# Groups of two images in place of four, two pursuit chains three steps apart, coefficients scattered by index

## What is computed

```python
g = sigmoid(gate)
x = x + conv2d(gn(x), tern(w), b) + g * conv2d(gn(x), tern(w_child), b_child)   # 3x3, per-channel norm
D = dictionary / (norm(dictionary, axis=0) + EPS)          # [512, 256]: 32 channels * 4 * 4, 256 atoms
X = patches of gn(x), 4x4, [512, 256 per image]
G = D.T @ D + DIAG_EPS * eye;  h_bar = h = (D.T @ X).T
for k in 1..5:
    index = argmax(abs(h) * ~mask)                         # greedy choice of an atom
    # one more row of a Cholesky factor, then the coefficients x_stack of the chosen atoms
    h = h_bar - x_stack @ G[I]
coeffs[b, I] = x_stack
x = x + fold(D @ coeffs)
```

## Time and profile of the kernel before

| | |
|---|---|
| median of 3 runs | 606.79 us |
| profiled execution | 606.02 us, span 604.2 us |
| VectorE busy | 522.8 us, 87% |
| TensorE busy | 457.3 us, 76%, mean granted clock 0.90 |
| ScalarE busy | 310.6 us, 51% |
| GpSimd busy | 222.0 us, 37% |
| chain that ended last | DVE 54%, PE 24%, issue 8% |

### The profile page before, as it was taken

The page is one execution under the profiler, slowest core; times in us unless marked ns, Lnnn a source line. Parts: engine busy times, 40 slices in busy tenths (PEclk is TensorE's granted clock), DMA queues, the critical chain, the costliest instruction groups (busy, mean ns, idle before and its releaser), DMA issues.

```text
span 604.2 us, 7708 instructions
## 1 busy us (share of the span) xinstructions
PE 457.3 (76%) x1778; PEld 319.7 (53%) x1778; DVE 522.8 (87%) x2507; ACT 310.6 (51%) x682; POOL 222.0 (37%) x269
## 2 busy tenths in 40 slices
PE   0198949897659587889985897999964646896955
PEld 0034935365558344567873445677942535674643
DVE  4493579999999999999998999989988999989980
ACT  3544564874662757656576495557122523452212
POOL 3000045243004756471036655620347375404330
PEclk9999988998889699999997897989985877898868
DMA  6979024986000368640304241121113111211113
GB/s 105 172 116 147 17 61 90 163 136 109 1 1 17 88 140 145 118 94 27 70 2 104 69 104 36 35 71 35 36 47 91 36 54 53 69 36 35 35 36 69
DMA packets 108189, 43.40 MB, mean 72 GB/s; under 512 B 103408, under 2 KB 103920, under 8 KB 108144
## 3 DMA queue, kind: packets, MB, share of 16 engines
q1 hardware_dynamic: 102000, 26.13, 25.8%
q0 software_dynamic: 6144, 16.79, 10.7%
HBM read 34.24 MB, written 8.65 MB: 71 GB/s over the span
## 4 chain that ended last, share of the span: by engine, by line
DVE 54%; PE 24%; issue 8%; SPq 4%; ACT 4%; DMA 3%; POOL 1%; DVEq 0%
PE h L395 13%; DVE picked L1054 11%; DVE junk L967 10%; DVE junk L964 9%; PE back_ps L395 7%; DVE top_i L912 7%; DVE top L906 4%; PE conv_ps L395 4%; SPq L246 3%; DMA rows<-gram,idx_u 1%; DVE mask L979 1%; ACT diag L637 1%; POOL rows L352 1%; SPq L253 1%; DMA d_sb<-in_L_conv_dictionary 1%
## 5 line engine op out<-in xcount | busy, mean ns | idle before, releaser
L395 PE MATMUL h<-rows,diag 128*128 128x256 f32 x640 | 173.8, 435 | 85.9 <-ACT diag L637 54.7
L352 POOL DMA_INDIRECT rows<-gram,idx_u x128 | 128.6, 1005 | 215.2 <-DVEq L952 185.6
L395 PEld LDWEIGHTS h<-rows,diag 128*128 128x128 f32 x640 | 137.8, 220 | 124.9 <-DMA rows<-gram,idx_u 58.4
L366 POOL TENSOR_TENSOR picked<-picked 128x256 f32<-128x256 f32 x120 | 88.4, 740 | 146.2 <-DVEq L1058 139.0
L637 ACT ACTIVATE diag<-ident,dx 128x128 f32<-128x128 f32 x320 | 96.8, 389 | 62.9 <-DVEq L1041 49.6
L628 ACT ACTIVATE score<-h 128x512 f32<-128x512 f32 x80 | 47.3, 594 | 113.5 <-PE h L395 103.7
L1054 DVE TENSOR_SCALAR picked<-iota,idx_last,x_last 128x256 f32<-128x256 f32 x160 | 85.3, 569 | 1.5 <-DVE picked L1054 0.9
L967 DVE SCALAR_TENSOR_TENSOR junk<-mask,rows 128x256 bf16<-128x256 bf16 x224 | 82.5, 434 | 0.0
L906 DVE MAX8 top<-score 128x8 f32<-128x256 f32 x160 | 64.5, 415 | 16.5 <-ACT score L628 13.2
L395 PE MATMUL h<-d_sb,z 128*128 128x256 f32 x256 | 63.2, 408 | 9.2 <-DVEq L897 8.3
L395 PEld LDWEIGHTS h<-d_sb,z 128*128 128x128 f32 x256 | 61.1, 328 | 11.4 <-issue 9.2
(11 more groups left out here) (148 smaller groups left out, 580.9 us busy)
## 6 DMA issues: line engine op xcount, KB each, us to landing
xa<-in_x SPq DMA_DIRECT2D x64, 128.0 KB
out<-x SPq DMA_DIRECT2D x64, 128.0 KB
xb<-in_x SPq DMA_DIRECT2D x42, 128.0 KB
rows<-gram,idx_u POOLq DMA_INDIRECT x128
xb<-in_x SPq DMA_DIRECT2D x14, 120.0 KB
rows<-in_x SPq DMA_DIRECT2D x6, 128.0 KB, 4.2
d_sb<-in_L_conv_dictionary SPq DMA_DIRECT2D x4, 128.0 KB, 3.8
gram<-coef_t SPq DMA_DIRECT2D x1, 256.0 KB, 2.2
```

The costliest lines, as they stand in the source:

```text
L352: pool.indirect_dma_start(out=rows[s][:, k, t, :], out_offset=None, in_=gram_dram[:, :], in_offset=bass.IndirectOffsetOnAxis(ap=idx_u[s][: ...
L366: last = nc.gpsimd.tensor_tensor(picked[:, m % 2, t, 0, :], picked[:, m % 2, t, 0, :], picked[:, m % 2, t, j, :], ALU.add)
L395: return nc.tensor.matmul(dst, lhs, rhs, start=start, stop=stop, skip_group_check=skip)
```

## The change

Images go in 8 groups of two; group g is in chain g % 2. The two chains are no longer at the same step: a list `ORDER` of (g, k), which all engines follow, has (g,2) (g+1,0) (g,3) (g+1,1) (g,4) (g+1,2) (g+2,0) (g+1,3) and so on, with two steps of the first group alone at the start and two of the last alone at the end. Front work of group g+2 and back work of group g-3 hang on the entries of the list.

The rows of coefficients (L1054), their sums (L366), their transposes and their copy are gone, except for the last group, whose rows are built by DVE and transposed as before. Instead, DVE computes a place for each coefficient, and POOL writes the coefficients to a zeroed matrix in DRAM with 20 indirect DMAs for each of 7 groups, one coefficient for each of 128 patches (`scatter`). SP zeroes that matrix (`store_zeros`) and loads it already transposed (`load_coef`). 

The convolution's result is kept as `x1[:, image, column mod 4, patch]`, so that `out_conv` writes with a stride and `correlate` and `reconstruct` read without one; 12 images are kept, and results go out through a buffer `y` of two images. The sums of the norms of group g+1 (second norm) and g+3 (first norm) are taken in one call and copied from PSUM by ACT (`copy_sums`). `select` looks at k+1 candidates instead of 8. The gathered rows have a semaphore for each tile, for which `update` and `extract` wait tile by tile. Two images instead of four are prepared before the first correlate, and the dictionary is loaded after the first two.

The core of the diff:

```diff
-    IMG_R = 4
-    ROUNDS = IMAGES // IMG_R
+    SLOTS = 2
+    PAIR = 2
+    GROUPS = IMAGES // PAIR
+    RING = SLOTS * PAIR
+    KEPT = 12
...
+    even = [(g, k) for g in range(0, GROUPS, 2) for k in range(STEPS)]
+    odd = [(g, k) for g in range(1, GROUPS, 2) for k in range(STEPS)]
+    ORDER = even[0:2]
+    for i in range(len(odd) - 2):
+        ORDER += [even[i + 2], odd[i]]
+    ORDER += odd[len(odd) - 2:]
+    LAST = GROUPS - 1
...
+        coef_dram = nc.dram_tensor("coef", [IMAGES * PLACES, 1], F32, kind="Internal").ap()
...
+            for g, k in ORDER:
+                front, back = g + 2, g - 3
+                if k == 0:
+                    load_after(2 * front + RING)
+                    if back >= 0:
+                        store(2 * back)
+                    store_zeros(g + 2)
+                elif k == 1:
+                    load_after(2 * front + 1 + RING)
+                    if back >= 0:
+                        store(2 * back + 1)
+                    if g >= 2:
+                        load_coef(2 * (g - 2))
+                elif k == 2 and g == LAST:
+                    store(2 * (g - 2))
+                    store(2 * (g - 2) + 1)
+                elif k == 3 and g == LAST:
+                    load_coef(2 * (g - 1))
+                elif k == 4 and g >= 1:
+                    load_coef(2 * (g - 1) + 1)
...
+            def scatter(g, first, last):
+
+                s, r = g % 2, g // 2
+                pool.wait_ge(x_last_ready[s], r + 1)
+                pool.wait_ge(zeros_stored[s], 16 * (r + 1))
+                for i in range(first, last):
+                    t, j = divmod(i, STEPS)
+                    pool.indirect_dma_start(out=coef_dram[:, :],
+                                            out_offset=bass.IndirectOffsetOnAxis(ap=place[s][:, t, j:j + 1], axis=0),
+                                            in_=x_last[s][:, t, j:j + 1], in_offset=None
+                                            ).then_inc(scattered[2 * s + t // 2], 16)
...
-                        if behind and (s, k) in sums_after:
-                            sum_picked(r - 1, sums_after[s, k])
-                sum_picked(r, 0)
-
-            sums_after = {(1, 0): 1, (0, 2): 2, (0, 3): 3}
-            body(0, False)
-            for r in range(1, ROUNDS):
-                body(r, True)
-            sum_picked(ROUNDS - 1, 1)
-            sum_picked(ROUNDS - 1, 2, (0,))
-            sum_picked(ROUNDS - 1, 3, (0,), 1)
+            for g, k in ORDER:
+                if k < STEPS - 1:
+                    gather(g, k)
+                if k == 1 and g >= 2:
+                    scatter(g - 2, 8, 11)
+                elif k == 2 and g >= 1:
+                    scatter(g - 1, 0, 4)
+                elif k == 3 and g >= 1:
+                    scatter(g - 1, 4, 8 if g < LAST else TILES * STEPS)
+                elif k == 4 and 1 <= g < LAST:
+                    scatter(g - 1, 11, TILES * STEPS)
...
+            def update(g, k):
+
+                s, r = g % 2, g // 2
                 for t in range(TILES):
-                    pe.wait_ge(diag_ready[s], TILES * (r * (STEPS - 1) + k) + t + 1)
+                    pe.wait_ge(rows_in[s][t], 16 * ((STEPS - 1) * r + k + 1))
+                    pe.wait_ge(diag_ready[s], TILES * ((STEPS - 1) * r + k) + t + 1)
...
-                            res = x1[:, n, c:PIX:PATCH]
+                        mm(back_ps[half][:, c2, :], ident[:, :], x1[:, n % KEPT, 2 * half + c2, :], c2 == 0, False, True)
+                    if q == 0:
+                        if n < PAIR * LAST:
+                            pe.wait_ge(coef_loaded[n % RING], 16 * (n // RING + 1))
...
+            for g, k in ORDER:
+                front, back = g + 2, g - 3
+                if k < STEPS - 1:
+                    update(g, k)
+                if k == 0:
+                    if g == 0:
+                        sums(1, None)
+                    elif g < LAST:
+                        sums(g + 1, g + 3 if g + 3 < GROUPS else None)
+                    if front < GROUPS:
+                        conv(2 * front)
+                    if back >= 0:
+                        reconstruct(2 * back)
+                elif k == 1:
+                    if front < GROUPS:
+                        conv(2 * front + 1)
+                    if back >= 0:
+                        reconstruct(2 * back + 1)
+                    if g == 0:
+                        correlate(1)
+                        pe.wait_ge(x1_done, 2 * (2 * front + 1) + 2)
+                        sums(None, 3)
+                elif k == 2 and g == LAST:
+                    reconstruct(2 * (g - 2))
+                    reconstruct(2 * (g - 2) + 1)
+                elif k == 3 and g == LAST:
+                    reconstruct(2 * (g - 1))
+                    reconstruct(2 * (g - 1) + 1)
+                elif k == 4 and front < GROUPS:
+                    correlate(front)
+            for m in range(PAIR):
+                tail_transposes(m)
+            for m in range(PAIR):
+                reconstruct(PAIR * LAST + m)
...
+            def out_back(n):
+
+                dst = y[:, n % 2, :].rearrange("p (n c) -> p c n", c=PATCH)
+                if n >= 2:
+                    act.wait_ge(y_stored[n % 2], 16 * PATCH * (n // 2))
...
+            scores(0, 0)
+            x_statistics(5)
+            out_conv(2)
+            square_sum(2)
+            copy_sums(None, 2, sums_h[1])
+            diags(0, 0)
+            out_conv(3)
+            square_sum(3)
+            root(None, 2)
+            scores(0, 1)
+            norm_x(4)
+            norm_x(5)
+            copy_sums(1, None)
+            out_conv(4)
+            square_sum(4)
+            root(1, None)
+            diags(0, 1)
+            norm_y(2)
+            norm_y(3)
+            scores(0, 2)
+            out_conv(5)
+            square_sum(5)
+            x_statistics(6)
+            x_statistics(7)
+            scores(1, 0)
+            x_statistics(8)
+            copy_sums(None, 3)
+            root(None, 3)
...
+            for g, k in ORDER[2:]:
+                front, back = g + 2, g - 3
+                if k == STEPS - 1:
+                    if front < GROUPS:
+                        scores(front, 0)
+                    for n in (2 * (g + 4), 2 * (g + 4) + 1):
+                        if n < IMAGES:
+                            norm_x(n)
+                    if 2 * (g + 5) < IMAGES:
+                        x_statistics(2 * (g + 5))
+                    continue
+                diags(g, k)
+                if k == 0:
+                    if g == 1:
+                        norm_x(6)
+                        norm_x(7)
+                    scores(g, 1)
+                    if g < LAST:
+                        copy_sums(g + 1, g + 3 if g + 3 < GROUPS else None)
+                    if front < GROUPS:
+                        out_conv(2 * front)
+                        square_sum(2 * front)
+                    if back >= 0:
+                        out_back(2 * back)
+                elif k == 1:
+                    if g < LAST:
+                        norm_y(2 * (g + 1))
+                        norm_y(2 * (g + 1) + 1)
+                    scores(g, 2)
+                    if front < GROUPS:
+                        out_conv(2 * front + 1)
+                        square_sum(2 * front + 1)
+                    if back >= 0:
+                        out_back(2 * back + 1)
+                elif k == 2:
+                    scores(g, 3)
+                    if 2 * (g + 4) + 1 < IMAGES:
+                        x_statistics(2 * (g + 4) + 1)
+                    if g == LAST:
+                        out_back(2 * (g - 2))
+                        out_back(2 * (g - 2) + 1)
+                else:
+                    if g + 1 < LAST:
+                        root(g + 2, g + 4 if g + 4 < GROUPS else None)
+                    scores(g, 4)
+                    if g == LAST:
+                        out_back(2 * (g - 1))
+                        out_back(2 * (g - 1) + 1)
+            for m in range(PAIR):
+                copy_tail(m)
+            for m in range(PAIR):
+                out_back(PAIR * LAST + m)
...
+            def variance(yg, xg):
+
+                nonlocal vars_made
+                vars_made += 1
+                dve.wait_ge(sums_done, vars_made)
...
+            def norm_params(yg, xg):
+
+                nonlocal params_made
+                params_made += 1
+                dve.wait_ge(root_done, params_made)
...
+                seen = k + 1
...
+                    c = step(v.scalar_tensor_tensor(out=place[s][:, :, :], in0=idx_u[s][:, :, :].rearrange("p j t -> p t j"),
+                                                    scalar=float(PATCHES), in1=first, op0=ALU.mult, op1=ALU.add))
...
-                    if j == k - 1:
-                        dve.wait_ge(rows_in[s][j], 16 * TILES * (r + 1))
...
-            def scatter(r, m):
-
```

(42 more changed lines are left out.)

884 lines of the change are left out of this document (366 added, 518 removed).

## The result

| | before | after |
|---|---|---|
| median | 606.16 us (604.25 to 607.86) | 648.59 us (647.21 to 650.45) |
| profiled execution, span | 604.2 us | 648.6 us |
| VectorE busy | 522.8 us | 439.0 us |
| TensorE busy, mean granted clock | 457.3 us, 0.90 | 448.8 us, 0.86 |
| time at the lower of the two clock levels | 120 us in 16 stretches | 179 us in 28 stretches |

The change makes the kernel slower: the ratio is 1.07, 95% interval 1.0669 to 1.073. I had said 614 with a range up to 640, so the sign came as forecast and the time lies outside the range.

What follows compares the result with a forecast made beforehand. VectorE was taken to set the pace in the rounds, TensorE close behind. Start 145, half periods 355.5 and the end gave 592.8 us; 20 for the clock made 612.8, 1.8 around the span 614.6, given as 614, range 572 to 640.

Steps and rivals of the forecast that it cites:

- A scatter: GpSimd's 140 coefficient writes, estimated from the gather at 1.25 us each, in slots where they cost nothing.
- The first scan: Start of the kernel: with two images prepared instead of four, it comes at 58.7 us, not 67.5.
- The wait for copy_sums in (0,2): In the start, DVE's extract of group 0, step 2 waits 10.7 us for copy_sums in ACT's queue.
- (B): Rival, slower by GpSimd: from 2.1 us a scatter it becomes the bound; at 2.5, 662 us; chance 0.07.
- The walk of the queues: Middle of the kernel, engine by engine in program order at full clock: six half periods sum to 355.5 us against 381.
- half periods: Stretches from the scan of (g,4) to that of (g+1,4), g=0 to 5, walked at 54 to 65 us.
- The two places where DVE stands: In the half period g=2: 9 us for scores at the third maximum, 5 us for the root in (g+2,1).
- (A): Rival, faster: queues do not hold DVE as walked, each half 55.5 us, half the clock loss; 582 us, chance 0.33.
- the clock's: TensorE's lower granted clock after pauses, two in each half; with start and end 12 x 1.7 = 20 us.
- the full-clock sum 592.8: Whole kernel before the clock's loss: start to 145, halves to 500.5, then the end to 592.8 us.
- the terms from 526.1 on: End of the kernel, after (7,2): bare updates, steps (7,3) and (7,4) and solves, put at 567.1 us.
- (C): Rival, no change: half of the stalls and the clock's low end of 10 us; 605 us, chance 0.10.

Runs made afterwards that it cites:

- the run with one scatter: Kernel after with one of five coefficient scatters of each tile, 28 instead of 140, loads and zero stores kept: 648.68 us, ratio 1.0695.
- out_back moved: Kernel after with unread matmuls in TensorE's pauses, less five behind the k=0 reconstruction, and slot k=0's out_back behind the next step's root on ScalarE: 609.97 us.
- the run with norm_x moved: Kernel after with norm_x of two images and one statistics pass moved on ScalarE behind the scores of step 2: 656.78 us, ratio 1.0833.
- the first fill: Kernel after with 406 more matmul records, whose results nobody reads, in TensorE's pauses: 612.85 us, ratio to before 1.0112.
- the long fill: Kernel of the first fill with more unread matmuls in the start, behind update k=2 of group 0 and at the end: 721.66 us.

## Why the prediction was right and wrong

**The terms that held.** A scatter was taken at 1.25 us: 0.991 and 0.30 between them, 1.29. An x1 matmul takes 395 ns. The first scan was put at 58.7: 58.5. The wait for copy_sums in (0,2) was 10.7: 10.6. norm_x and statistics 7.9: 7.8. (B) needed 2.1 us a scatter and is dead by size; the run with one scatter shows that fewer of them would have given nothing.

The Trainium skill, DMA: Bandwidth & Descriptors, section Specifications, has transfers under 512 B done as read-modify-write. In the kernel after, the scatters of 4 bytes land 2.2 us after their issue and the gathers of 1 KB 2.8 us, so no slowness of that kind shows:

```profile
coef<-x_last,place POOLq DMA_INDIRECT x140, 2.2
rows<-gram,idx_u POOLq DMA_INDIRECT x128, 2.8
```

**The walk of the queues held.** At full clock it gave half periods of 58.5, 62, 65, 60.5, 55.5 and 54. With the pauses filled they are 60.2, 62.6, 69.3, 60.9, 55.8 and 53.9, five of six within 2 us. The sixth, g=2, still has a low clock in it (0.95), and with out_back moved it is 62.8. The two places where DVE stands are those named: 10.0 us at the third maximum of g=2 (9 walked) and 8.8 at the root (5 walked, with convolution, sums and reconstruction before it at the low clock). This also settles (A): with TensorE at 0.95 to 1.00 the middle halves still take 60 to 69 us and not 55.5, so the waits come from program order. And the run with norm_x moved shows that the 7.8 us can't be moved to the one other place that was tried.

**The term that failed is the clock's.** I put it at 12 pauses x 1.7 = 20 us. The fill gives back 35.7 and doesn't reach both ends; the full-clock sum 592.8 and the measured span 648.6 leave 55.8. Where it went: start 8.9 ((0,4) at 153.9 for 145), the half periods 38.2, the end 8.7.

- Of the halves 31 are clock, by the first fill, and most of the 7 that remain lie in g=2 (4.3), whose clock was still 0.95.
- Of the start's 8.9, 3.4 are luck of the profiled execution, for the run with one scatter, the same up to there, has 150.4 without any fill. About 3.5 more are clock: (0,4) comes at 146.9 and 147.0 in the two kernels with the long fill. With two of its three fills in the start it comes at 149.7.
- Of the end only 3 are clock: with the fill there it goes from 101.0 to 97.9. Of the other 5 to 6, 2.5 are a slot (6,4) of 16.2 for 13.65 us, in which the third maximum waits for scores that stand behind a reconstruction, and 1.8 are a slip: the terms from 526.1 on, as listed, add up to 568.9 and not to 567.1, so the sum should have been 594.6.

So some 38 of the 55.8 were seen to be clock, against 20, and the rest is smaller items of the walk.

Two errors stand behind the 20. First the count: I took two pauses in a half, and there are four of 2.3 to 9.5 us: ahead of updates k=2, k=0, k=3 and k=1, each in front of an update that waits for its diagonals, as the walk itself shows when it is read on TensorE's side. The time at the low level went from 120 to 179 us, in 28 stretches for 16. Second the price: the earlier trace rows is one stretch of 6.9 us with TensorE at work for 4.08 of it, 2.0 lost. Two other updates of g=2 in the kernel after, which ran at the low level for most of their time:

```profile
290.67 6.14 PE L415 MATMUL h<-rows,diag 128*128 128x256 f32 x16 [3.91 <-ACT diag L679]
...
335.45 2.64 PE L415 MATMUL h<-rows,diag 128*128 128x256 f32 x8 [3.25 <-ACT diag L679]
```

The same half in the kernel with fill and out_back moved has the clock at 1.00 throughout, and gives the price: update k=1 6.14 us for 3.69 there, update k=2 8.33 for 5.42, update k=0 2.64 for 1.97, sums and convolution 8.7 for 6.0. Together 8.7 us, where I had assumed 3.4; the half took 9.6 over the walk (74.6 for 65).

**The range.** The prediction doesn't add up its upper end of 640. It lies 26 us above the forecast, and the clock's term alone was 18 short. The clock was one number, taken from one row of a kernel in which such a loss was hidden. The excess grew with the very stalls that I forecast, and the two should have had one range. (C) was wrong in the same term; its 605 also holds the whole walk, although it speaks of half of the stalls. (B)'s 662 is nearer in time than the forecast, but its mechanism is not there.

**What the change lost.** DVE does 84 us less. In the old order, with a fifth of the rows and no sums, DVE's busy time fell by nearly as much, from 522.8 to 441.3, and this was worth 41 us. The new order makes TensorE and ScalarE the chain (PE 24% to 51%), and there low clock counts.

## What to carry to other kernels

Taking work off the busiest engine is worth little more than its distance to the next one while both are in use; here a round had 8 us between DVE and PE and gained 7. When an order leaves TensorE pauses of 2 to 10 us, four in a half period of 75, its low clock must be priced per pause by the work that stands right behind it, and whether that work is on the path decides whether it counts at all. And a block that is moved in an engine's queue takes its wait along: look at who waits for what stands behind the new place.

## What the runs showed that I had not expected

Work that nobody needs can make a kernel faster: 406 matmul records more took 35.7 us off. The Trainium skill, TensorE: Matmul & The Clock Gate, Part 1, says that the ramp penalty is under 1% of a typical kernel span. It says so of the warm-up that a kernel's first matmuls pay; low stretches after pauses come on top, and here their fill gives back 5.5%, in the old order nothing net, so what they cost depends on where they lie.

A signal from TensorE can reach ScalarE 2 to 14 us late while GpSimd issues scatters: 80 us in one execution of 718. It came in three of the ten kernels with fill and all scatters, in all of their timed runs, and not in the one of the three that was also run with a fifth of the scatters. The three ran on one chip and all others with fill on other chips, so neither the scatters nor the fill is shown to be the cause.
